# Two layers of linear attention and mixture of experts: order of ScalarE's work in the first experts, and the form of the second layer's first logits

## What is computed

```python
xn = _layernorm(x)
x = x + L0_attn(xn) + L0_ffn(xn)      # elu linear attention, 16 heads; 8 silu experts of 176 + a shared one
xn = _layernorm(x)
x = x + L1_attn(xn) + L1_ffn(xn)      # causal elu attention, 8 heads, rms norm, gate; 8 gelu experts of 512

# routing, both layers
logits = xn @ gate.T                   # 8 a token
topw, topi = top_k(softmax(logits), 2)
wdense[token, topi] = topw / topw.sum()
# experts of layer 0
eo = (silu(xn @ wg[e]) * (xn @ wu[e])) @ wd[e]
y = sum_e wdense[:, e] * eo
```

## Time and profile before

| | |
|---|---|
| median of three runs | 1013.43 us (1011.47 to 1016.01) |
| profiled execution, its own time | 1015.37 us |
| its span | 1013.8 us, 22330 instructions |
| busy: TensorE, VectorE, GpSimd, ScalarE | 866.2, 693.8, 619.8, 568.5 us |
| DMA | 190.67 MB, mean 188 GB/s |
| chain that ended last, by engine | PE 51%, VectorE 15%, ScalarE 8%, DMA 8%, SyncE's queue 7%, issue 7% |
| first experts | about 254 to 462 us of the span |

### The profile page before, as it was taken

How to read it: one execution, slowest core, us unless ns; L and a number is a source line. 1 busy time by engine, 2 the same in 40 slices (tenths; PEclk the granted TensorE clock), 3 DMA queues, 4 the chain that set the end, 5 groups by cost and what they waited for, 6 DMA issues and landing times.

```text
span 1013.8 us, 22330 instructions
## 1 busy us (share of the span) xinstructions
PE 866.2 (85%) x7923; PEld 768.6 (76%) x7923; DVE 693.8 (68%) x1800; ACT 568.5 (56%) x1184; POOL 619.8 (61%) x607
## 2 busy tenths in 40 slices
PE   4799899899798897976887979977689999998982
PEld 4688788798788887864665656655489999997982
DVE  6878877855566886592788797787455656666764
ACT  4755654343555547455866666654256666655550
POOL 2256767666016665474776767884777777565554
PEclk9999999999799999897998998997889999999997
DMA  9699961131678887561111111112737777798985
GB/s 269 216 407 395 394 255 48 45 87 51 214 239 270 274 266 217 176 216 58 36 36 28 35 33 37 41 45 69 276 115 257 259 266 264 242 312 317 305 300 153
DMA packets 130510, 190.67 MB, mean 188 GB/s; under 512 B 15872, under 2 KB 85504, under 8 KB 130272
## 3 DMA queue, kind: packets, MB, share of 16 engines
q1 hardware_dynamic: 95520, 139.90, 40.7%
q0 software_dynamic: 16832, 34.77, 10.7%
q10 hardware_dynamic: 18048, 14.58, 4.8%
HBM read 110.47 MB, written 80.84 MB: 189 GB/s over the span
## 4 chain that ended last, share of the span: by engine, by line
PE 51%; DVE 15%; ACT 8%; DMA 8%; SPq 7%; issue 7%; POOL 4%; ACTq 0%; DVEq 0%; POOLq 0%
PE pair L824 9%; DMA ex_stage<-in_experts 6%; PE pair L691 3%; PE pair L771 3%; PE pair L770 3%; PE pair L772 3%; PE pair L918 3%; ACT a_rows L1535 3%; PE pair L941 2%; POOL sent L1837 2%; PE pair L801 2%; PE pair L611 2%; PE pair L869 2%; SPq L490 2%; PE pair L949 2%
## 5 line engine op out<-in xcount | busy, mean ns | idle before, releaser
L1837 POOL DMA_INDIRECT sent<-a_rows,slot x224 | 221.2, 988 | 100.1 <-issue 53.6
L1848 POOL DMA_INDIRECT ex_joined<-outs,slot x128 | 130.5, 1019 | 128.3 <-PE pair L763 81.0
L1934 POOL DMA_INDIRECT back<-ex_tile_out,address x142 | 152.6, 1074 | 77.9 <-DVE ex_tile_out L1367 40.1
L1653 ACT ACTIVATE ex_w_hi<-ex_stage 128x768 fp32r<-128x768 f32 (+1 forms) x72 | 67.8, 942 | 153.8 <-DMA ex_stage<-in_experts 144.1
L770 PE MATMUL pair<-ex_x_hi,ex_w_hi 128*128 128x256 f32 x497 | 148.8, 299 | 0.2
L1319 DVE TENSOR_TENSOR ex_w_lo<-ex_stage,ex_w_hi 128x768 fp32r<-128x768 f32 (+1 forms) x72 | 77.6, 1078 | 102.8 <-ACT ex_w_hi L1653 102.7
L771 PE MATMUL pair<-ex_x_lo,ex_w_hi 128*128 128x256 f32 x497 | 142.4, 286 | 0.0
L772 PE MATMUL pair<-ex_x_hi,ex_w_lo 128*128 128x256 f32 x497 | 142.2, 286 | 0.0
L824 PE MATMUL pair<-ex_stage,ex_hid 128*128 128x128 f32 x1136 | 132.5, 275 | 0.0
L824 PEld LDWEIGHTS pair<-ex_stage,ex_hid 128*128 128x128 f32 x1136 | 129.9, 192 | 0.0
L1678 ACT ACTIVATE ex_hid<-pair,ex_stage 128x256 f32<-128x256 f32 x284 | 107.4, 496 | 0.5 <-PE pair L772 0.4
(11 more groups left out here) (239 smaller groups left out, 2086.4 us busy)
## 6 DMA issues: line engine op xcount, KB each, us to landing
ex_stage<-in_experts SPq DMA_DIRECT2D x72, 578.0 KB
outs<-v_heads SPq DMA_DIRECT2D x8, 4352.0 KB, 33.7
ex_stage<-in_experts SPq DMA_DIRECT2D x72, 320.0 KB
ex_tile_in<-sent SPq DMA_DIRECT2D x72, 128.0 KB
outs<-ex_tile_out SPq DMA_DIRECT2D x71, 128.0 KB, 2.4
ex_joined<-back ACTq DMA_DIRECT2D x16, 512.0 KB, 6.5
ex_tile_in<-sent SPq DMA_DIRECT2D x54, 132.0 KB
X<-in_x SPq DMA_DIRECT2D x16, 256.0 KB, 5.4
```

The source lines that it names most:

```text
L1837: pool.indirect_dma_start(out=sent[layer], out_offset=bass.IndirectOffsetOnAxis(ap=slot_i[layer][k][:, s, j:j + 1], axis=0), in_=rows[laye ...
L1848: pool.indirect_dma_start(out=joined[g % NJOIN][:, j, k, :], out_offset=None, in_=outs, in_offset=bass.IndirectOffsetOnAxis(ap=slot_i[0][k ...
L1934: pool.indirect_dma_start(out=back, out_offset=bass.IndirectOffsetOnAxis(ap=address[i % NSIDE][:, s // HALF, s % HALF:s % HALF + 1], axis= ...
```

## The change

In ScalarE's loop over the first layer's tiles, the rounding of tile n+1's weights is put ahead of the copy of tile n-2's results; the rounding of rows stays behind the copy. Second, the logits of the second layer's first four groups are made by columns in iteration 28, copied by ScalarE into a part of the old transposed tokens (`sums_ex`), and transposed back in iteration 29. Third, routing of the first supergroup goes over iterations 30 to 36 in place of 30 to 33, and its count of ranks moves from 32 to 33.

```diff
-EX_LOGITS, EX_EXPS, EX_RANKS = 28, 31, 32
-EX_ROUTE = {30: "ab", 31: "c", 32: "de", 33: "fgh"}
+EX_SUMS, EX_LOGITS, EX_EXPS, EX_RANKS = 28, 29, 31, 33
+EX_ROUTE = {30: "a", 31: "b", 32: "c", 33: "d", 34: "ef", 35: "g", 36: "h"}
...
-    return step > 1 and (step in LOGITS[layer] or layer == 1 and LEAD + 2 <= step < NG + LEAD + 2)
+    return step > 1 - layer and (step in LOGITS[layer] or layer == 1 and LEAD + 2 <= step < NG + LEAD + 2)
...
+        sums_ex = flat(xTg(GPS))
...
             def next_layer(n):
 
-                if n in EX_COLUMNS or n in (EX_LOGITS, EX_RANKS):
+                if n in EX_COLUMNS or n in (EX_SUMS, EX_LOGITS, EX_RANKS):
                     pe.wait_ge(x_lo_here, min(n + 2, NTILES))
...
+                if n == EX_SUMS:
+                    logits_by_columns(1, 1, 0).then_inc(sums_done, 1)
                 if n == EX_LOGITS:
-                    logits(1, LOGITS[1][1], logits_bank(1, 1))
+                    sums_to_rows(6, 0, GPS, sums_ex).then_inc(logits_done, GPS)
...
             for n in range(NTILES + 1):
+                if n + 1 < NTILES:
+                    split_weights(0, n + 1)
                 if n >= 2:
                     results0(n - 2)
                 if n + 1 < NTILES:
-                    split_weights(0, n + 1)
                     split_rows(0, n + 1, 6)
...
+                if n == EX_SUMS:
+                    keep_sums(1, 1, 0, GPS * P, sums_ex)
```

More of the change, by code:

```diff
@@ L581, in logits_by_columns, with sums_to_rows @@
                 return m
-            def sums_to_rows(b, c, n):
+            def sums_to_rows(b, c, n, src=sums_t):
                 for k in range(n):
-                    m = pe.transpose(bank[b][:, c + k * P:c + (k + 1) * P], sums_t[:, c + k * P:c + (k + 1) * P], ident)
+                    m = pe.transpose(bank[b][:, c + k * P:c + (k + 1) * P], src[:, c + k * P:c + (k + 1) * P], ident)
                 return m
@@ L842, in next_layer_read @@
                     pe.wait_ge(xT_ready, NG + EX_COLUMNS[n] + 1)
+                if n == EX_SUMS:
+                    pe.wait_ge(sums_here, sums_upto(1, 1))
                 if n == EX_LOGITS:
@@ L1547, in keep_logits, with keep_sums @@
                     act.wait_ge(chosen, layer * NS + s - 1)
-                if step == 1:
+                if layer == 0 and step == 1:
                     src = blocks(bank[b][:, 0:E * n], E)
                 else:
-                    c = P * layer
+                    c = P * layer if step > 1 else 0
                     src = blocks(bank[b][:, c:c + NARROW * n], NARROW)[:, :, 0:E]
                 act.activation(logit[s % 2][:, a:a + n, :], src, ACT.Copy).then_inc(logits_here, len(groups))
-            def keep_sums(layer, step, a, b):
+            def keep_sums(layer, step, a, b, dst=sums_t):
                 act.wait_ge(sums_done, sums_upto(layer, step))
-                act.activation(sums_t[:, a:b], bank[logits_bank(layer, step)][:, a:b], ACT.Copy).then_inc(sums_here, 1)
+                act.activation(dst[:, a:b], bank[logits_bank(layer, step)][:, a:b], ACT.Copy).then_inc(sums_here, 1)
             def exponentials(layer, s):
```

## The result

The changed kernel takes 1060.77 us (median of 4 runs, 1057.37 to 1065.13), the kernel before beside it 1012.62. The ratio is 1.0459, with a 95% interval of 1.0426 to 1.0492: 4.6% slower. The forecast was 1065.

A forecast was written before the change was run, and what follows sets the result against it. ScalarE's wait for the weights' load was taken to bound the kernel. With the new order, 4 steps of 7.0 and 27 of 7.4 us give 227.8 where 176.1 stood, +51.7, so 1065 us; range 1049 to 1084.

The forecast's parts named there:

- The circle: First experts: load of tile n+2 cannot be issued before that of n+1 has landed; 31 steps cost +51.7 us.
- 1.35 us for the rounding and the copy: ScalarE, each step: rounding start to next start 0.75 us, then the copy of results 0.60 us.
- 1.77 from copy to issue: SyncE, each step: end of the copy of results to issue of the weights' load, 1.77 us.
- The load: Issue of the weights' load to the rounding waiting for it: 3.9 us for tiles 5 to 8, then 4.3.
- quiet rows: Profile rows of the kernel before where the load runs without gathers: 3.95 and 3.80 us from issue to rounding.
- the rival: TensorE idles 2.7 us per tile and its clock falls: 8.4 us for 27 tiles, 1092 us; chance 0.10.
- Part 2: Second layer's logits by columns: saves about 5 us at the old pace, worth nothing more in the circle.
- Part 3: Routing over seven tiles, same instructions later: price 0, bounds -3 and +1 us.

The follow-up runs named there:

- part 1 alone: Kernel before with only the rounding of the next tile's weights moved ahead of the copy of results: 1063.23 us, ratio 1.0474.
- part 2 alone: Kernel before with only the logits of the first four groups by columns, old ScalarE order and routing: 1084.55 us beside 1088.82, ratio 0.9961.
- parts 2 and 3 alone: Changed kernel with the old order on ScalarE, keeping logits by columns and routing over seven tiles: 1008.23 us, ratio 0.9935 to the kernel before.

## Why the prediction was right

**The circle.** It is the step that carried the forecast, and the runs bear it out four ways: part 1 alone makes the loss, opening the circle at SyncE removes it with the order unchanged, a copy put into it costs its length in every step in the new order and about a third of that in the old (on another chip), and a shorter load makes every step shorter.

**Its terms.** 1.35 us for the rounding and the copy was 0.75 + 0.58; 1.77 from copy to issue was 1.77. The load was mis-sized: 3.9 without gathers was 3.7 on average over four steps (3.66 in the rows above), and 4.3 beside the gathers was 4.0 (27 steps from 304.41 to 496.37 are 7.11 us each, less 3.1). The predicted 227.8 us for 31 steps were 219.5, 8.3 too much. That the forecast of 1065 us came within 5 us of 1060.77 is therefore in part luck: 1.9 us that it put at nothing were lost outside the steps, and the medians of the two kernels lie 48.2 us apart where the traced executions lie 45.2. I had split the difference between quiet rows and rows at a DMA rate of 267 GB/s; at the new pace the engines move 199 GB/s (first row below), and the load takes little more than alone. The Trainium skill's page "DMA: Bandwidth & Descriptors", section "Anatomy of one DMA", gives 2.0 us plus bytes at 436 GB/s, an estimate of 3.5 us here. That is nearer the 3.66 of the quiet row than my 3.9. But the section measures single DMAs issued by GpSimd, and here SyncE issues two, so the nearness shows little.

**TensorE's clock.** It did fall in pauses, as the rival had it. The windows of the changed kernel (busy us of each engine, then granted clock, DMA share, GB/s) and one down group behind a pause:

```profile
345.00:381.00 36.00, 24.72 (x194) 23.71 (x194) 21.96 (x55) 13.82 (x25) 15.89 (x17) 0.95 0.64 199
```

```profile
333.72 2.95 PE L804 MATMUL pair<-ex_stage,ex_hid 128*128 128x128 f32 x16 [2.19 <-ACT ex_tile_out L1693]
```

The 16 products took 2.95 us in place of 2.02, and next time, behind a pause of 1.43, 2.05. From 345 to 381 us the clock was 0.95, and before it was 1.00. But each lowered group fits into the slack: in every one of the 31 steps the copy follows the rounding without a wait for TensorE, so the circle's terms make up the whole step and nothing is left for the clock. This is read from the trace; no run changed the clock alone.

**Part 2.** Predicted at most 1.7 us for the columns, under 1 for the transposes and about 5 us saved at the old pace. TensorE in the changed kernel:

```profile
456.58 1.08 PE L576 MATMUL pair<-xT,gates 128*32 128x128 f32 x32 [0.15 <-DVE ex_x_lo L1332]
457.59 2.05 PE L804 MATMUL pair<-ex_stage,ex_hid 128*128 128x128 f32 x16
...
463.81 0.66 PE L589 MATMUL pair<-consts,xT 128*128 128x128 f32 x4 [1.58 <-DVE ex_x_lo L1332]
```

1.08 in place of 5.20, and the down products behind them 2.05 in place of 3.76. The run of part 2 alone gave 4.3 us for it, and in the circle it gave nothing except that the old form sticks out there by 3.4 us in one tile. The down products behind the old logits were slow at a lowered clock. Windows of the end of the logits and the down products behind them, first in the kernel before, then in the changed kernel:

```profile
416.00:420.00 4.00, 4.00 (x20) 4.00 (x20) 1.39 (x7) 0.28 (x1) 0.00 (x0) 0.50 0.36 108
```

```profile
457.00:460.00 3.00, 3.00 (x46) 2.80 (x38) 2.87 (x15) 0.65 (x2) 0.95 (x1) 1.00 0.84 254
```

TensorE is busy throughout both. Yet behind the old form, with 32 moving columns to a product, the granted clock is 0.50, the lower of its two levels, and behind the new one it is 1.00.

**Part 3.** The price of 0 missed the end of the loop. Pieces e to g now stand between the last tiles' hidden products on VectorE, when there is no longer a load to hide them. ScalarE waits there:

```profile
502.68 0.38 ACT L1675 ACTIVATE ex_gate_s<-pair 48x256 f32<-48x256 f32 x1 [2.23 <-DVE ex_hid L1359]
```

The stretch from the last rounding to attention is 1.5 us longer, against a bound of +1. With part 1 alone, where the new order stands and the pieces are over sooner, that stretch is 9.57 us (501.15 to 510.72), 2.4 less than the 11.99 of the changed kernel. This supports the reading; no run moved the pieces alone in the new order.

## What to carry to other kernels

When an instruction is put ahead of another on an in-order engine, ask what its wait now holds up, and follow the semaphore of the instruction that moved back: if it releases the buffer for the next transfer, and the wait is for the last one, the number of buffers no longer matters and the transfers run one by one. Such a circle has a price that can be summed before it is built, from the rows of a kernel that hasn't got it. The slack to look for is between the release and the engine that uses it (0.76 us in one tile here, and none in those where SyncE already waited), not the idle time of the engine that is reordered. And a buffer should be released by what last reads it, not by a later step: with the load waiting for the down products, either order gives 1007 to 1008 us. It removes the loss of the new order and gives nothing in the old one, since parts 2 and 3 alone already give 1008.23.

## What the hardware showed that I had not expected

The same kernel before took 1013.8 us on one chip and 1088.8 on others. The traces on the latter are those of other versions of the kernel. The instructions themselves are as long there, but there are pauses of several us that more than one engine shares and that no semaphore explains. In the run of part 2 alone, between 396 and 399.6 us, VectorE and ScalarE do nothing and TensorE is busy for 0.93 us (window: busy us of TensorE, its weight loads, VectorE, ScalarE, GpSimd, then clock, DMA share, GB/s):

```profile
396.00:399.60 3.60, 0.93 (x3) 0.49 (x3) 0.00 (x0) 0.00 (x0) 1.61 (x2) 0.84 0.39 113
```

ScalarE's next row:

```profile
399.62 0.60 ACT L1693 ACTIVATE ex_tile_out<-pair 128x512 f32<-128x512 f32 x1 [7.13 <-remote]
```

VectorE's next instruction starts at 400.98, after 5.41 us of idle time. The cause of these pauses is open. What they teach is to compare only within one chip.
